# Token attention's scores modulated straight from PSUM, and 13 of 16 norms normalised by ACT, in a fused four-block transformer kernel

## What is computed

```python
x = x + attn_a(layernorm(x))   # 8 heads over channels: softmax of a 16x16 similarity per head
x = x + ffn(layernorm(x))      # routed mixture: 8 experts, hidden 336
x = x + attn_b(layernorm(x))   # one head over tokens, with modulated scores
x = x + ffn(layernorm(x))      # the same mixture, same weights
```

## Time and profile before

| | us |
|---|---|
| median of 3 runs | 535.79 |
| lowest and highest | 533.95, 536.09 |
| the profiled execution's own time | 532.75 |
| its span (first to last instruction) | 531.0 |
| mean granted TensorE clock in the span | 0.99 |
| DVE, POOL, ACT busy | 348.6, 291.2, 239.2 |

### The profile page before, as it was taken

The page is one execution under the profiler, slowest core; times in us unless marked ns, Lnnn a source line. Parts: engine busy times, 40 slices in busy tenths (PEclk is TensorE's granted clock), DMA queues, the critical chain, the costliest instruction groups (busy, mean ns, idle before and its releaser), DMA issues.

```text
span 531.0 us, 6553 instructions
## 1 busy us (share of the span) xinstructions
PE 495.8 (93%) x2128; PEld 349.3 (66%) x2128; DVE 348.6 (66%) x769; ACT 239.2 (45%) x399; POOL 291.2 (55%) x280
## 2 busy tenths in 40 slices
PE   6797989999996997998989999899998999999996
PEld 6665756776664665766757777577775677666663
DVE  3649483775699797568785699956989354653332
ACT  3386326246622735423836248462383523523221
POOL 4346794238578092734565357553564544655553
PEclk9999999999999998999999999989999899999999
DMA  8600000000000000000000000000000000000000
GB/s 248 200 0 2 0 2 0 1 0 2 1 0 1 0 1 1 0 2 0 2 0 1 0 0 2 0 1 1 21 1 0 1 21 0 1 2 20 0 1 20
DMA packets 7917, 7.38 MB, mean 14 GB/s; under 512 B 716, under 2 KB 7756, under 8 KB 7884
## 3 DMA queue, kind: packets, MB, share of 16 engines
q1 hardware_dynamic: 7884, 6.97, 4.3%
HBM read 5.91 MB, written 1.05 MB: 13 GB/s over the span
## 4 chain that ended last, share of the span: by engine, by line
PE 63%; DVE 16%; issue 4%; ACT 2%; POOL 1%; DVEq 0%; POOLq 0%; ACTq 0%
PE bank L1085 20%; PE bank L949 12%; PE bank L951 11%; PE bank L950 11%; PE bank L1136 3%; DVE t L883 2%; DVE xn L735 2%; PE bank L1124 1%; DVE mk L909 1%; PE bank L1053 1%; DVE mk L908 1%; DVE mk L913 1%; DVE gt L843 1%; DVE mk L912 1%; DVE ge L837 1%
## 5 line engine op out<-in xcount | busy, mean ns | idle before, releaser
L530 POOL TENSOR_TENSOR t<-t,sl 128x512 f32<-128x512 f32 x105 | 136.3, 1303 | 123.0 <-DVE t L883 120.5
L633 ACT ACTIVATE sl<-bank 128x512 f32<-128x512 f32 x168 | 99.9, 597 | 182.8 <-PE bank L951 147.6
L1085 PE MATMUL bank<-t,WD 128*128 128x512 f32 x336 | 168.1, 595 | 0.8 <-ACT YT L639 0.8
L883 DVE TENSOR_TENSOR t<-bank,sbc 128x512 f32<-128x512 f32 x105 | 71.9, 685 | 77.0 <-PE bank L951 76.8
L949 PE MATMUL bank<-xhF,WGh 128*128 128x512 f32 x168 | 100.5, 598 | 2.7 <-ACT sl L633 2.0
L530 POOL TENSOR_TENSOR t<-t,sbc 128x512 f32<-128x512 f32 x63 | 81.6, 1326 | 6.0 <-ACT sbc L627 5.9
L1085 PEld LDWEIGHTS bank<-t,WD 128*128 128x128 f32 x336 | 63.7, 190 | 27.8 <-issue 13.8
L949 PE MATMUL bank<-xhF,WUh 128*128 128x512 f32 x168 | 68.4, 407 | 7.7 <-DVE t L883 7.7
L883 DVE TENSOR_TENSOR t<-bank,sl 128x512 f32<-128x512 f32 x63 | 42.7, 684 | 43.7 <-ACT sl L633 25.8
L951 PE MATMUL bank<-xhF,WUl 128*128 128x512 f32 x168 | 67.1, 399 | 0.0
L951 PE MATMUL bank<-xhF,WGl 128*128 128x512 f32 x168 | 67.0, 399 | 0.0
(11 more groups left out here) (180 smaller groups left out, 688.3 us busy)
## 6 DMA issues: line engine op xcount, KB each, us to landing
stage<-in_gate SPq DMA_DIRECT2D x7, 192.0 KB, 6.1
stage<-in_up SPq DMA_DIRECT2D x7, 192.0 KB, 6.3
WD<-in_down SPq DMA_DIRECT2D x7, 192.0 KB, 6.2
X<-in_x SPq DMA_DIRECT2D x4, 256.0 KB, 5.5
out<-X SPq DMA_DIRECT2D x4, 256.0 KB, 2.3
raw<-in_small SPq DMA_DIRECT2D x1, 388.0 KB, 4.6
raw<-in_small SPq DMA_DIRECT2D x1, 192.0 KB, 2.7
rows<-in_row SPq DMA_DIRECT2D x1, 136.0 KB
```

What stands on the lines that cost most here:

```text
L530: pool.tensor_tensor(t2[k % NT2][:, :], t2[k % NT2][:, :], by[:, :], ALU.mult).then_inc(a_done, 1)
L633: act.activation(sl[k % NSL][:, :], bank[k % 2][:, :], ACT.Silu).then_inc(silu_done, 1)
L883: dve.tensor_tensor(t2[k % NT2][:, :], bank[2 + k % 2][:, :], by[:, :], ALU.mult).then_inc(t2_done, 1)
L1085: pe.matmul(OACC[:, :], WD[:, c, :], t2[k % NT2][:, :], start=(c == 0), stop=(c == CH - 1))\
```

## The change

Scores: the copy of the score tile to SBUF by ACT goes. DVE reads the bank in PSUM: two masks, two mask-and-add instructions, one that combines the jumps with the first threshold, one that multiplies by the scores and takes the maximum of the row in the same pass while writing `Sb`, and a negation of the 128x1 maximum. The bank is freed by the sixth of these. The plan counts the bank as taken until part 3 of `bsp`. Norms: from the fourth in the order (`DVE_NORMS = 3`) ACT writes xn as Identity of rstd * X - mean * rstd; POOL makes the negated mean and its product with rstd. The tables of steps and costs are changed with it: the token attention thread ends at offset 30 in place of 35, some steps of the others move by one.

```diff
--- before.py
+++ after.py
@@ -47,6 +47,7 @@
...
+DVE_NORMS = 3
@@ -75,7 +76,7 @@
...
-A_STEPS = [(0, "stats"), (1, "xn"), (3, "ag"), (4, "xT"), (5, "ar"), (7, "asim"), (8, "ass"), (9, "ascale"),
+A_STEPS = [(0, "stats"), (1, "xn"), (4, "ag"), (4, "xT"), (5, "ar"), (7, "asim"), (8, "ass"), (9, "ascale"),
@@ -85,17 +86,17 @@
...
-B_STEPS = [(0, "stats"), (2, "xn"), (4, "xT"), (4, "xl"), (6, "bqk", 0), (7, "bqk", 1), (7, "bqkl", 0),
-           (7, "bqkl", 1), (10, "bs", 0), (10, "bsp", 0, 0), (11, "bsp", 0, 1), (13, "bsp", 0, 2),
-           (15, "bs", 1), (14, "bsp", 0, 3), (15, "bsp", 1, 0), (16, "bv"), (15, "bsp", 1, 1),
-           (17, "bsp", 1, 2), (18, "bs", 2), (18, "bsp", 1, 3), (19, "bsp", 2, 0), (19, "bexp", 0),
-           (19, "bexp", 1), (20, "bsp", 2, 1), (21, "bsp", 2, 2), (22, "bs", 3), (25, "bsp", 2, 3),
-           (22, "bsp", 3, 0), (25, "bsp", 3, 1), (26, "bsp", 3, 2), (27, "bsp", 3, 3), (28, "bexp", 2),
-           (27, "bexp", 3), (30, "bpT", 0), (31, "bpT", 1), (30, "bpT", 2),
-           (32, "bpT", 3), (34, "bo", 0), (34, "bo", 1), (35, "bo", 2), (35, "bo", 3), (35, "byx")]
-F_STEPS = [(0, "stats"), (1, "xn"), (3, "xT"), (4, "xl"), (6, "route"), (7, "rexp"), (7, "inner", 0),
-           (10, "inner", 1), (9, "rsum"), (12, "rrank"), (12, "tanh"), (12, "gelu"), (14, "act"),
-           (14, "actk"), (18, "sbc")]
+B_STEPS = [(0, "stats"), (2, "xn"), (4, "xT"), (5, "xl"), (7, "bqk", 0), (8, "bqk", 1), (8, "bqkl", 0),
+           (8, "bqkl", 1), (11, "bs", 0), (11, "bsp", 0, 0), (12, "bsp", 0, 1), (12, "bsp", 0, 2), (13, "bsp", 0, 3),
+           (14, "bs", 1), (14, "bsp", 1, 0), (15, "bsp", 1, 1), (15, "bsp", 1, 2), (16, "bsp", 1, 3),
+           (17, "bexp", 0), (17, "bexp", 1), (17, "bs", 2), (17, "bsp", 2, 0), (18, "bsp", 2, 1),
+           (18, "bsp", 2, 2), (19, "bsp", 2, 3), (20, "bs", 3), (20, "bsp", 3, 0), (21, "bv"),
+           (21, "bsp", 3, 1), (21, "bsp", 3, 2), (22, "bsp", 3, 3), (23, "bexp", 2), (23, "bexp", 3),
+           (25, "bpT", 0), (26, "bpT", 1), (26, "bpT", 2), (27, "bpT", 3),
+           (29, "bo", 0), (29, "bo", 1), (30, "bo", 2), (30, "bo", 3), (30, "byx")]
+F_STEPS = [(0, "stats"), (1, "xn"), (4, "xT"), (5, "xl"), (6, "route"), (7, "rexp"), (7, "inner", 0),
+           (10, "inner", 1), (9, "rsum"), (12, "rrank"), (12, "tanh"), (13, "gelu"), (15, "act"),
+           (15, "actk"), (18, "sbc")]
@@ -111,11 +112,11 @@
...
-COST = dict(stats=(0, 0, 1.2), xn=(0, 0, 1.1), xT=(.4, .5, 0), xl=(0, 0, .6), ag=(.9, .3, 0), ar=(.5, .4, .4),
+COST = dict(stats=(0, 0, 1.2), xn=(0, 1.2, 0), xT=(.4, .5, 0), xl=(0, 0, .6), ag=(.9, .3, 0), ar=(.5, .4, .4),
...
-            sbc=(.4, .5, 0), yT=(.4, 0, .6), bqk=(.7, 1, 0), bs=(.7, .5, 0), bsp=(0, 0, .9),
+            sbc=(.4, .5, 0), yT=(.4, 0, .6), bqk=(.7, 1, 0), bs=(.7, 0, 0), bsp=(0, 0, 1.2),
@@ -202,6 +203,8 @@
...
+            if s[0] == "bs":
+                by = ("bsp",) + s[1:] + (3,)
@@ -313,6 +316,8 @@
...
+        nms = [sb(f"nm{i}", [P, NT]) for i in range(2)]
+        nmrs = [sb(f"nmr{i}", [P, NT]) for i in range(2)]
@@ -348,10 +353,11 @@
...
-        mk = [sb(f"mk{i}", [P, T], BF16) for i in range(4)]
+        mk = [sb(f"mk{i}", [P, T], BF16) for i in range(2)]
...
+        bmp = sb("bmp", [P, NT])
@@ -377,6 +383,7 @@
...
+        xn_act = sem("xn_act")
@@ -403,6 +410,13 @@
...
+        def wait_xn(eng, seq):
+            if seq < DVE_NORMS:
+                eng.wait_ge(xn_ready, seq + 1)
+            else:
+                eng.wait_ge(xn_act, seq - DVE_NORMS + 1)
@@ -479,12 +493,18 @@
...
-                        pool.wait_ge(xn_ready, seq - 1)
+                        wait_xn(pool, seq - 2)
...
+                    if seq >= DVE_NORMS:
+                        pool.tensor_scalar(nms[seq % 2][:, :], mv[:, :, 0], -1.0, None, ALU.mult)
...
-                    pool.tensor_tensor(rstd[:, :], rt[:, :], nhalf[:, :], ALU.pow).then_inc(rstd_ready, 1)
+                    r = pool.tensor_tensor(rstd[:, :], rt[:, :], nhalf[:, :], ALU.pow)
+                    if seq >= DVE_NORMS:
+                        chain(r)
+                        r = pool.tensor_tensor(nmrs[seq % 2][:, :], nms[seq % 2][:, :], rstd[:, :], ALU.mult)
+                    r.then_inc(rstd_ready, 1)
@@ -537,6 +557,15 @@
...
+                if kind == "xn" and norm_no[s[1:]] >= DVE_NORMS:
+                    _, what, b = s
+                    seq = norm_no[what, b]
+                    wait_full(act, xT_turn[seq - 2])
+                    act.wait_ge(rstd_ready, seq + 1)
+                    for i in range(NT):
+                        r = act.activation(xns[seq % 2][:, i, :], X[:, NT * (b % NB) + i, :], ACT.Identity,
+                                           bias=nmrs[seq % 2][:, i:i + 1], scale=rstds[seq % 2][:, i:i + 1])
+                    r.then_inc(xn_act, 1)
@@ -654,13 +683,6 @@
...
-                if kind == "bs":
-                    _, b, i = s
-                    t = turn_of[s]
-                    wait_full(act, t)
-                    if b:
-                        wait_full(act, turn_of["bpT", b - 1, NT - 1])
-                    act.activation(Sb[:, i, :], m_bank(t)[:, :], ACT.Copy).then_inc(n_free(t), 1)
@@ -717,13 +739,15 @@
...
+                    if seq >= 2:
+                        dve.wait_ge(rstd_ready, seq - 1)
...
-                if kind == "xn":
+                if kind == "xn" and norm_no[s[1:]] < DVE_NORMS:
@@ -901,24 +925,29 @@
...
-                    x_ = Sb[:, i, :]
-                    step_no = 3 * (NT * b + i)
+                    t = turn_of["bs", b, i]
+                    x_ = m_bank(t)[:, :]
+                    jumps, first = mk[0], mk[1]
...
-                        wait_free(dve, turn_of["bs", b, i])
-                        dve.tensor_scalar(mk[0][:, :], x_, X10 / 10, 2.0, ALU.is_ge, ALU.mult)
-                        chain(dve.tensor_scalar(mk[1][:, :], x_, X25 / 10, 7.0, ALU.is_ge, ALU.mult))
-                        dve.tensor_tensor(mk[0][:, :], mk[0][:, :], mk[1][:, :], ALU.add).then_inc(mk_ready, 1)
+                        wait_full(dve, t)
+                        dve.tensor_scalar(jumps[:, :], x_, X25 / 10, 2.0, ALU.is_ge, ALU.mult).then_inc(mk_ready, 1)
+                        dve.tensor_scalar(first[:, :], x_, X10 / 10, 0.5, ALU.is_ge, ALU.add).then_inc(mk_ready, 1)
...
-                        dve.tensor_scalar(mk[2][:, :], x_, X85 / 10, 5.0, ALU.is_gt, ALU.mult)
-                        chain(dve.tensor_scalar(mk[3][:, :], x_, X95 / 10, 5.0, ALU.is_gt, ALU.mult))
-                        dve.tensor_tensor(mk[2][:, :], mk[2][:, :], mk[3][:, :], ALU.add).then_inc(mk_ready, 1)
+                        dve.wait_ge(mk_ready, 5 * (NT * b + i) + 1)
+                        dve.scalar_tensor_tensor(jumps[:, :], x_, X85 / 10, jumps[:, :], ALU.is_gt, ALU.add).then_inc(mk_ready, 1)
+                        dve.wait_ge(mk_ready, 5 * (NT * b + i) + 3)
+                        dve.scalar_tensor_tensor(jumps[:, :], x_, X95 / 10, jumps[:, :], ALU.is_gt, ALU.add).then_inc(mk_ready, 1)
...
-                        dve.wait_ge(mk_ready, step_no + 2)
-                        chain(dve.tensor_tensor(mk[0][:, :], mk[0][:, :], mk[2][:, :], ALU.add))
-                        dve.scalar_tensor_tensor(x_, mk[0][:, :], 1.0, x_, ALU.add, ALU.mult).then_inc(mk_ready, 1)
+                        dve.wait_ge(mk_ready, 5 * (NT * b + i) + 4)
+                        dve.scalar_tensor_tensor(jumps[:, :], jumps[:, :], 2.5, first[:, :], ALU.mult, ALU.max).then_inc(mk_ready, 1)
...
-                        dve.wait_ge(mk_ready, step_no + 3)
-                        dve.tensor_reduce(bmx[:, i:i + 1], x_, AX_X, ALU.max, negate=True).then_inc(sp_ready, 1)
+                        dve.wait_ge(mk_ready, 5 * (NT * b + i) + 5)
+                        if b:
+                            wait_full(dve, turn_of["bpT", b - 1, NT - 1])
+                        dve.tensor_tensor_reduce(Sb[:, i, :], jumps[:, :], x_, 2.0, -3e38, ALU.mult, ALU.max, bmp[:, i:i + 1])\
+                           .then_inc(n_free(t), 1)
+                        wait_free(dve, t)
+                        dve.tensor_scalar(bmx[:, i:i + 1], bmp[:, i:i + 1], -1.0, None, ALU.mult).then_inc(sp_ready, 1)
@@ -962,7 +991,7 @@
...
-                    pe.wait_ge(xn_ready, norm_no[what, b] + 1)
+                    wait_xn(pe, norm_no[what, b])
@@ -975,7 +1004,7 @@
...
-                    pe.wait_ge(xn_ready, norm_no["A", b] + 1)
+                    wait_xn(pe, norm_no["A", b])
```

## The result

The changed kernel took 521.37 us (median; 520.62 to 522.18, 4 runs) against 534.87 us for the kernel before, measured beside it. The ratio is 0.9751, interval 0.9713 to 0.9788: 2.5% faster. The forecast was 520.5 us.

The account below looks back on a forecast made before the run. TensorE bounds the kernel, held up mainly by DVE; gains of 14.6 and 5.1 us less costs of 2.6 and 3.2 give 13.9, so 532.75 becomes 518.9, 521.9 by the median; forecast 520.5 us, range 509 to 534.

Parts of the forecast that it names:

- What bounds it: TensorE's pace; the ledger of weight-load waits and three clock dips puts what DVE can give back at 26.4 us.
- no slice below 0.95 clock: Sign that the forecast is right: TensorE's granted clock shows no slice below 0.95 after the change.
- Norms: 13 norms' xn move to ACT: 33.5 us off DVE, 0.40 us per ACT instruction, 1.6 us a norm.
- Scores: DVE's score group: 4.69 us a tile instead of 5.9, saving 20 us; DVE's total falls to about 295.
- The readers of PSUM stay flat: DVE's four PSUM-reading score instructions per tile don't contend with POOL and stay near 0.685 us each.
- Case B: Rival: new scores gain nothing (4.3 us uncontended against 4.69), only xn helps; gain 7.6, 525 to 528 us; chance 0.20.
- Rstd: POOL's added negation and product: rstd 0.6 us later per norm; ACT's waiting charged 0.2 us a norm, 2.6 us.
- Banks: Score bank held about 6 us until the maximum instruction; 0.2 us charged for each of 16 tiles, 3.2 us.
- Case C: Rival: held score bank delays TensorE 1.3 us per tile, 21 us; slower, 536.7 (profiled) or 539.7 us (median); chance 0.10.
- Plan: Step tables: attention threads five chunks shorter, some steps one later; each thread had slack, no cost charged.
- The sum: Gains 14.6 (to 210 us) and 5.1 (second stretch), less 2.6 and 3.2: 13.9 us; 518.9 profiled, 521.9 median.
- The hq waits: Most waits from 210 to 420 us, at the router chain's end; little won, so half of 7.6+2.6: 5.1.

Follow-up runs that it names:

- run 4: Changed kernel, but ACT copies the scores to SBUF as before and the seven DVE instructions read them there; 534.08 us, ratio 0.9986 to the kernel before.
- run 1: Kernel before with only the change's step tables (A_STEPS, B_STEPS, F_STEPS), all instructions as they were; 545.52 us, ratio 1.020.
- run 3: Changed kernel with all 16 norms back on DVE (DVE_NORMS = 16), same order of steps; 529.27 us, ratio 0.9898 to the kernel before.
- run 8: Changed kernel with the fourth norm, at 47 us, back on DVE (DVE_NORMS = 4); 519.65 us, ratio 0.9755 to the kernel before.
- run 10: Changed kernel with later token attention thread starts (51, 70 for 48, 67) and the fourth norm on DVE; 510.09 us, ratio 0.9553 to the kernel before.
- run 6: Changed kernel with every xn put one chunk later in the order; 520.39 us, ratio 0.9762 to the kernel before.
- run 11: Changed kernel with thread starts 51 and 70, fourth norm on DVE and xn one chunk later; 512.70 us, ratio 0.9598 to the kernel before.
- run 7: Changed kernel with the first mask of each tile computed twice, 11 us more of DVE; 524.22 us, ratio 0.9829 to the kernel before.
- run 9: The changed kernel as it is, measured again on another occasion; 521.66 us, ratio 0.9765 to the kernel before.

## Why the prediction was right, and where it was right by luck

**What bounds it.** Right. The ledger of the earlier trace rows was the right place to look: the listed waits for DVE fell from 26.3 to 2.3 us, and no TensorE instruction changed. The sign "no slice below 0.95 clock" failed: two stretches at the lower level are there, at new places (0.58 and 0.61 over 4 us), both behind stalls for ACT.

**Norms.** 33.5 us off DVE and 1.6 us a norm on ACT. Measured: four xn take 1.65 us. By itself one takes 0.48, above my 0.40, but they overlap.

**Scores.** Forecast 4.69 us a tile; measured 67.8/16 + 0.08 + 0.15 = 4.47. The pass with the maximum is one pass, 0.68 and a readout of 0.08, where I had taken 0.8; the combination's mean is 0.91 where I had 0.95. DVE's total was to be 295 and is 297.0. The new scores and norms save 23.2 and 33.5 us, 56.7 in all, and DVE's total fell by 51.6. The other 5 us are hardly work that came back: added up line by line, DVE's busy time falls by 57.5 us (372.7 to 315.2), and the router's instructions about cancel (gt<-gt,ge falls from 0.88 to 0.75 us, ge<-ge,tri rises from 0.42 to 0.62, hq<-hq,xa from 0.75 to 0.94). The total counts time only once where the records of neighbouring instructions overlap, and there is less of such overlap after the change.

**The readers of PSUM stay flat.** Right (660 to 693 ns). Run 4 shows that the form matters and not the number of instructions: the same seven from SBUF are stretched to as much as 1.83 us and the gain is gone, though ACT's copies have a part in that. The rule of the Trainium skill that the prediction cites (SBUF — State Buffer, Who interferes with whom) agrees with the lines shown of run 4 and of the changed kernel. Case B is refuted by runs 1 and 3: in the new tables the new scores are worth 3.0 points. The advice of the Trainium skill's page VectorE: DVE Perf Modes (Rules for kernel authors) to copy to SBUF first if there are many operations doesn't hold here: following it is run 4, 2.2 points slower.

**Rstd.** 0.6 us later was right: from the end of the statistics to the release of xn at 45 us it was 1.4 us in the kernel before and 2.0 after. I charged 2.6 us for ACT's waiting, spread over 13 norms. What is shown is one norm, the one at 47 us, that cost 3 to 4 us with its clock (runs 8 and 10); for the others runs 6 and 11 give no price, since the later xn brought waits of its own.

**Banks.** 3.2 us were charged. TensorE is never seen to wait for the bank's release, and run 7 bounds what DVE's time is worth at a third. Case C is refuted.

**Plan.** This step failed: I put the new tables at nothing. Run 1 shows them at 11 us slower on the old instructions; with them, the changes of scores and norms had 24 us to give and not 14. The flaw is in taking slack in the offsets as slack in the engines: the four parts of `bsp` were drawn together, and I didn't cost what an already full DVE does with a denser table. Part of that price stands in the changed kernel too: the stall for YT, 5.4 us with a dip of 1.6, is in every trace with the new B_STEPS and the old starts (3.7 to 4.2 us the longest, in runs 1, 3, 4 and 6 to 9) and in none with the old B_STEPS (at most 0.8 us). The new tables gave something as well, the waits for hq.

**The sum.** 19.7 us won less 5.8 of costs made 13.9; measured by the spans of the two traces it is 10.6, by the medians 13.5. Both terms were too small. In the first stretch DVE's waits came back nearly whole, 14.5 of 14.5. In the second the listed waits fell by 6.1 of 7.6 net, but 1.5 of that are still idle under "issue" in front of `act`, so about 4.6. The three dips of 4.3 us went (I had nine tenths of the first stretch and half of the second). That makes 23.4 us. The hq waits were not DVE's backlog: run 1 lost them with DVE as full as before, so it was the new tables that took them, by which of their shifts is open. The forecast was right that they are no fault of the mk, and wrong to expect nothing of the tables. Against the 23.4 us stand stalls for which I had no term: YT behind the exponential pair, 3.7 and 1.65 us with a dip of 1.6, the fourth norm's 4.2 us with a dip of 1.7, 3 us of silu and 1.5 of YT in front of its transposes. These are 17.4 us; waits of the same kinds were 4.2 us in the kernel before, so 13 us are new, against my 5.8. By this rough account 23.4 less 13 is 10, near the 10.6 of the spans. So the forecast had the gain too small by 4 us and the costs by 7. That the forecast time was met within 1 us is chance: the two errors cancelled in part, and the rest is that the profiled executions lie differently to their medians (2.1 us below before, 0.8 above after).

## What to carry to other kernels

When two engines exclude each other, cost an instruction by its form and not by its best time: a DVE reader of PSUM at 0.69 us every time beat a reader of SBUF at 0.42 to 1.5. When the late engine is relieved, look for where, on the others, several long pieces (an exponential pair with its table loads) stand in front of the one short copy that frees the accumulator; taking one pair out of its way by later thread starts was worth half as much as the whole change. A hand-made table of steps belongs to the durations that it was made for, and has to be costed as a change of its own: run it alone, on the old instructions, before naming the cause of a new stall.

## What the runs showed of the hardware

- A scalar_tensor_tensor with both tensors in bf16 in SBUF takes 0.69 us for 128x512, as the one with an fp32 input does; the plain bf16 tensor_tensor takes 0.41. Bf16 brings this form nothing.
- Multiply with a running maximum in one pass takes 0.68 us and a readout of 0.08, where multiply and reduction were 0.69 and 0.67.
- A 128x128 Identity on ACT with both scale and bias from tensors takes 0.48 us, 0.18 more than a copy of that size; four in a row take 1.65 us.
- The exclusion can cost POOL, too: 7.6 us more for its 168 products in run 4.
- A stall's length alone doesn't tell what the clock does behind it. After 3.7 us without a matmul the granted clock was 0.61 over 4 us in the changed kernel, 1.7 us lost in all; after the same stall in run 8 3.4 us were lost. In the kernel before, TensorE stood 3.2 us at 164 to 167 us and the clock did not fall:

```profile
164.00:168.00 4.00, 0.78 (x4) 0.67 (x4) 3.96 (x5) 0.60 (x1) 4.00 (x4) 1.00 0.00 0
168.00:172.00 4.00, 2.68 (x10) 1.56 (x9) 3.96 (x5) 0.80 (x2) 2.36 (x2) 1.00 0.02 4
```
